# An interaction MLP in fp32 halves: rows loaded in 32-wide blocks and turned by VectorE, one spill and 16 gathers per chunk

## The chip, the cores and the metric

The kernel runs on one NeuronCore of one Trainium2 chip. The metric is the time of one execution on the device in microseconds (us), as the median over several runs. TensorE (PE) does matmuls and writes PSUM; VectorE (DVE), ScalarE (ACT) and GpSimd (POOL) do elementwise work; SyncE (SP) issues most transfers, which run on 16 DMA engines.

## The reference

It is the top of a recommendation model, for 2048 samples. Each sample has 27 feature rows of 128 numbers (`bottom_output`) and one dense row of 128.

```python
dots = jnp.einsum('bfd,bgd->bfg', bottom_output, bottom_output)
pairs = dots[:, _TRIL_I, _TRIL_J]                 # 351 = 27*26/2 per sample
x = jnp.concatenate([bottom_mlp_output, pairs, pad], axis=1)      # 128 + 351 + 1 = 480
for w, b in ((w0, b0), (w1, b1), (w2, b2), (w3, b3)):             # 480-1024-1024-512-256
    x = jax.nn.relu(x @ w.T + b)
y = x @ w_out.T + b_out                                           # 2048 x 1
```

Everything is float32.

## The kernel before

**Precision.** Each float32 operand is kept as two parts in the format fp32r: a high part (the value rounded) and a low part (value minus high part). A product is three matmuls: weight high with input high, weight high with input low, weight low with input high.

**Chunks.** The batch is cut into 8 chunks of 256 samples. A chunk has 16 units of 16 samples (4 groups of 4 samples). While chunk c goes through the layers, the units of chunk c+1 are prepared between its matmuls. The loop over c = 1 to 6 runs chunks of the same shape; chunk 0 also turns most of the weights, and chunk 7 prepares nothing.

**A unit, before.** SP loads 16 samples into a slot of `rows` (ring of 4): 108 partitions, one per (sample of the group, feature), with 4 x 128 numbers each (`load_rows`, L386). TensorE turns them by four transposes into a bank of `turned_ps` (`turn`, L546). ScalarE copies out the high part (`turned_hi`, L718), VectorE the low part (`turned_lo`, L828), into `xt`. Four Gram matmuls (`gram`, L602) give high x high and high x low of 4 samples at a time; of each 128x128 result the four diagonal 27x27 blocks count, one in each quadrant of 32 partitions. ScalarE copies quadrants 0 to 2 to `parts` (`gram_parts`, L730), VectorE quadrant 3 (`last_part`, L848). VectorE transposes the high x low part (`turn_low`, L862), and GpSimd adds the three terms (`add_parts`, L479 and L486) into `grams`.

**Spill and gather.** When the 16 units of a chunk are summed, SP writes the four quadrants of `grams` to DRAM (`blocks`), one transfer each (`spill`, L400), and then gathers the 351 pairs, one feature pair per partition, in the order of the reference: 28 transfers of 1 to 26 partitions with runs of 64 numbers (`gather_piece`, L346). Behind the gathers SP issues the rows of units 0 to 3 of the next chunk; the other 12 follow in the next chunk, each when the unit four before it is turned. ScalarE and VectorE split the gathered `pairs` into parts of the input tile x0 (`pairs_hi` L753, `pairs_lo` L904).

**The order within a chunk.** `chunk_steps` writes out one list of steps, which every engine walks in order. The steps "mm" are the products (`products`, L635), in tiles of m: 8 tiles of 12 matmuls in layer 0, 8 of 24 in layer 1, 4 of 24 in layer 2, 2 of 12 in layer 3, 408 in all. Each tile fills one of two banks of `acc`; ScalarE drains it with bias and ReLU into `h_full` (ring of 2; `drain`, L743) and VectorE splits that (`split`, L870 high and L872 low). A product group waits for the drain of the group two before it, a drain for the split of the one two before. Within layers 0 and 1 a hook comes after every HOOK = 9 matmuls; each takes the next entry of `unit_steps`: turn unit n, sum unit n-3, Gram of unit n-2. So 18 hooks end after 162 matmuls. In chunk 0 the hooks come every 6 matmuls, weights are turned in many of them, and the units' places start at hook 12. The step "pairs", the split of the next chunk's gathered pairs, stands ahead of layer 3; on ScalarE it lies ahead of the drains of layer 3. In layer 0 the first tile's product k waits for the part k of x0.

**The prologue.** Chunk 0's 16 units are turned and multiplied in plain float32 (`turn_early`, `gram_early`), W0's eight tile rows are turned by TensorE (L541) and split by ScalarE (L693, L694), then come spill and gather, 16 transfers on SP and 12 on ScalarE. W0 is loaded by two transfers of 0.96 MB.

**PSUM.** Eight banks: 2 for `acc`, 2 for `turned_ps`, 4 for Grams.

Of the kernel before, what the change touches and what calls it, by code (L numbers as in the profile page):

```python
# [14 lines left out]
P = 128  # L15
# [5 lines left out]
GROUP = 4  # L21
# [12 lines left out]
K_LAST = LAYERS[0][0] - 3 * P  # L34
# [49 lines left out]
def pair_pieces():  # L84


    out = []
    for a in range(1, FEATS):
        q, b = a * (a - 1) // 2, 0
        while b < a:  # L90
            n = min(a - b, P - (q + b) % P)
            out.append((a, b, n, q + b))
            b += n
    return out


PIECES = pair_pieces()
PIECES_OF = [sum(q // P == t for _, _, _, q in PIECES) for t in range(3)]


def unit_steps(n):


    steps, g = [], n - XT_LAG
    if n < UNITS:
        steps.append(("turn", n))
    if g >= 1:
# [25 lines left out]
def first_hooks():  # L133


    places = [FIRST_UNIT + 2 * i for i in range(4)] + [FIRST_UNIT + 8 + 4 * i // 3 for i in range(UNITS + XT_LAG - 4)]
# [11 lines left out]
def chunk_steps(gram, first=False):  # L148
# [4 lines left out]
    hooks = first_hooks() if first else [unit_steps(u) for u in range(UNITS + XT_LAG)] if gram else []  # L153
# [3 lines left out]
    for layer in range(3):  # L157
        for m in range(M_TILES[layer]):
# [4 lines left out]
            while k < K_TILES[layer]:  # L163
# [17 lines left out]
def dlrm_program(nc, x, x_mlp, w0, b0, w1, b1, w2, b2, w3, b3, w_out, b_out, y):  # L181
    weights = [w0, w1, w2, w3]
    biases = [b0, b1, b2, b3]
    with ExitStack() as ctx:
# [19 lines left out]

        h_a = sb("h_a", [P, 8, 2, CHUNK], F32R)
# [4 lines left out]
        rows = sb("rows", [P, ROWS_RING, UNIT_GROUPS, DIM])  # L210
        mlp_rows = sb("mlp_rows", [P, 2, P])
# [7 lines left out]
        stage_small = sb("stage_small", [24, P])  # L219
# [10 lines left out]
        w0_loaded = [sem(f"w0_loaded{i}") for i in range(2)]  # L230
# [7 lines left out]
        pairs_zeroed = sem("pairs_zeroed")  # L238
        xt_zeroed = sem("xt_zeroed")
# [4 lines left out]
        turned = sem("turned")  # L244
        xt_hi_done = sem("xt_hi_done")
# [4 lines left out]
        last_part_done = sem("last_part_done")  # L250
# [14 lines left out]
        weighted_done = sem("weighted_done")  # L265
# [7 lines left out]
        x_view = x.rearrange("(c u j s) f d -> c u (s f) j d", u=UNITS, j=UNIT_GROUPS, s=GROUP)  # L273
# [17 lines left out]
        out_bank = turned_ps[0:1, OUT_UNIT % TURN_RING, 0:CHUNK]  # L291

        def in_tile(layer, k, part):
            kk = K_LAST if layer == 0 and k == 3 else P
            src = x0 if layer == 0 else h_b if layer == 2 else h_a
            return src[0:kk, k, part, :]

        def weight(part, layer, m, k):
            kk = K_LAST if layer == 0 and k == 3 else P
            t = TILE0[layer] + m * K_TILES[layer] + k  # L300
            return part[0:kk, t * P:(t + 1) * P]
# [26 lines left out]

        def turned_cols(u):
# [41 lines left out]
        def _(sp):  # L371
# [6 lines left out]
            def load_rows(d, u):  # L378
# [13 lines left out]
            def spill(d):  # L392
# [56 lines left out]
            gather(0, [piece for i, piece in enumerate(PIECES) if i % 7 not in (1, 3, 5)])  # L449
# [15 lines left out]
        def _(pool):  # L465
# [5 lines left out]
            nc.gpsimd.memset(pairs[:], 0.0).then_inc(pairs_zeroed, 1)  # L471

            def add_parts(d, u):
# [4 lines left out]
                pool.wait_ge(last_part_done, n)  # L478
# [11 lines left out]
            def chunk(d):  # L490
                for u in range(UNITS):
                    add_parts(d, u)

            chunk(1)
            with pool.Fori(2, CHUNKS) as d:
                chunk(d)
# [3 lines left out]
        def _(pe):  # L500
            def turn_weights(n):
# [473 lines left out]
```

## Time and profile before

| | |
|---|---|
| median of 3 runs | 562.57 us (562.24 to 564.08) |
| profiled execution: own time | 563.71 us |
| profiled execution: span from first to last instruction | 561.9 us |
| granted TensorE clock, mean over the span | 0.989 |
| TensorE busy | 538.7 us (96%), 4521 matmuls |
| VectorE busy | 323.1 us (57%) |
| ScalarE busy | 295.5 us (53%) |
| GpSimd busy | 101.0 us (18%) |
| DMA packets | 76532, 47.49 MB, 15194 of them under 512 B |

Busy TensorE is a modelled value, since matmuls overlap: the time from one to the next is the better measure. Times of the trace are counted from the start of the span. In a row such as `205.84 1.08 PE acc L635 x9` the first number is the start and the second the length; L635 is line 635 of the kernel before.

### The profile page before, as it was taken

What the parts mean: (1) busy time and instruction counts of PE and PEld (TensorE: products, weight loads), DVE (VectorE), ACT (ScalarE), POOL (GpSimd) and SP (SyncE); (2) the same over time, 40 slices, a digit from 0 to 9 for tenths busy, and PEclk for the clock granted to TensorE, in tenths of its full rate; (3) what the DMA queues carried; (4) which work ended last, traced back from release to release, by engine and by line L of the source; (5) the groups of instructions that cost most, each with busy time, mean ns of one, the idle gap of its engine ahead of it and who ended that gap; (6) DMA issues with size and microseconds to landing.
All of it is one profiled execution on the core that took longest, in us unless ns stands there. A gap on an engine that the chain in (4) does not pass through costs nothing.

```text
span 561.9 us, 13936 instructions
## 1 busy us (share of the span) xinstructions
PE 538.7 (96%) x4521; PEld 531.7 (95%) x4521; DVE 323.1 (57%) x814; ACT 295.5 (53%) x740; POOL 101.0 (18%) x231
## 2 busy tenths in 40 slices
PE   6857999999999999999999999999999999999996
PEld 6847999999999999999999999999999999999996
DVE  3656878647842587237852588337862588325222
ACT  4535788528841588127841488227851488314112
POOL 0000044002430045002430044101430044100000
PEclk9996999999999999999999999999999999999999
DMA  9978131133213230233312231133311331100000
GB/s 233 278 268 273 43 111 40 61 93 112 81 54 81 66 112 29 65 86 98 91 53 59 75 116 37 62 89 90 99 51 37 93 111 47 59 20 2 1 1 1
DMA packets 76532, 47.49 MB, mean 85 GB/s; under 512 B 15194, under 2 KB 73850, under 8 KB 76506
## 3 DMA queue, kind: packets, MB, share of 16 engines
q1 hardware_dynamic: 75801, 47.00, 28.5%
q8 instruction: 15, 0.25, 0.2%
q10 hardware_dynamic: 705, 0.16, 0.2%
q14 instruction: 11, 0.09, 0.0%
HBM read 41.16 MB, written 5.98 MB: 84 GB/s over the span
## 4 chain that ended last, share of the span: by engine, by line
PE 82%; ACT 0%; DVE 0%; issue 0%; POOL 0%; ACTq 0%; POOLq 0%
PE acc L635 65%; PE gram_ps L602 9%; PE turned_ps L546 7%; PE gram_ps L541 1%; PE turned_ps L648 0%; PE turned_ps L611 0%; ACT parts L730 0%; ACT y_row L760 0%; DVE low_t L888 0%; ACT h_full L743 0%; DVE h_a L893 0%; POOL grams L486 0%; DVE h_a L891 0%; ACTq L728 0%; POOLq L482 0%
## 5 line engine op out<-in xcount | busy, mean ns | idle before, releaser
L635 PE MATMUL acc<-h_a,w_hi 128*128 128x256 f32 x1152 | 211.9, 284 | 0.0
L743 ACT ACTIVATE h_full<-acc,small_t 128x256 f32<-128x256 f32 x176 | 83.5, 474 | 182.2 <-PE acc L635 179.6
L635 PEld LDWEIGHTS acc<-h_a,w_hi 128*128 128x128 f32 x1152 | 179.1, 191 | 0.1
L635 PE MATMUL acc<-h_a,w_lo 128*128 128x256 f32 x576 | 162.9, 283 | 0.0
L730 ACT ACTIVATE parts<-gram_ps 27x216 f32<-27x216 f32 x336 | 114.4, 341 | 26.4 <-POOL grams L486 21.1
L635 PEld LDWEIGHTS acc<-h_a,w_lo 128*128 128x128 f32 x576 | 110.3, 192 | 0.0
L635 PE MATMUL acc<-x,w_hi 128*128 128x256 f32 (+1 forms) x512 | 99.5, 291 | 8.5 <-DVE x L904 8.5
L479 POOL TENSOR_TENSOR parts<-parts 128x128 f32<-128x128 f32 x112 | 52.3, 467 | 272.7 <-DVE parts L848 201.5
L635 PE MATMUL acc<-h_b,w_hi 128*128 128x256 f32 x512 | 93.4, 284 | 0.0
L635 PEld LDWEIGHTS acc<-x,w_hi 128*128 128x128 f32 (+1 forms) x512 | 80.0, 193 | 9.8 <-DVE x L904 8.7
L602 PE MATMUL gram_ps<-xt 128*128 128x256 f32 x448 | 80.1, 301 | 0.7 <-issue 0.6
L635 PEld LDWEIGHTS acc<-h_b,w_hi 128*128 128x128 f32 x512 | 79.7, 192 | 0.0
L828 DVE TENSOR_TENSOR xt<-turned_ps,xt 128x432 fp32r<-128x432 f32 x112 | 68.1, 608 | 18.3 <-ACT xt L718 16.0
L870 DVE CAST h_a<-h_full 128x256 fp32r<-128x256 f32 x96 | 28.9, 301 | 82.8 <-ACT h_full L743 82.2
L635 PE MATMUL acc<-x,w_lo 128*128 128x256 f32 (+1 forms) x256 | 72.9, 285 | 0.0
L635 PE MATMUL acc<-h_b,w_lo 128*128 128x256 f32 x256 | 72.4, 283 | 0.0
L718 ACT ACTIVATE xt<-turned_ps 128x432 fp32r<-128x432 f32 x112 | 59.3, 529 | 19.2 <-PE turned_ps L546 18.3
L870 DVE CAST h_b<-h_full 128x256 fp32r<-128x256 f32 x64 | 21.8, 340 | 82.1 <-ACT h_full L743 82.1
L486 POOL TENSOR_TENSOR grams<-parts,low_t 128x108 f32<-128x108 f32 x112 | 48.2, 430 | 106.4 <-DVE low_t L862 103.1
L546 PE MATMUL turned_ps<-ident,rows 108*128 108x108 f32 x464 | 62.2, 256 | 2.0 <-DMA rows<-in_r_bottom_output_dram 1.7
L602 PEld LDWEIGHTS gram_ps<-xt 128*128 128x128 f32 x448 | 60.4, 190 | 1.9 <-issue 1.9
L546 PEld LDWEIGHTS turned_ps<-ident,rows 108*128 108x128 f32 x464 | 49.7, 140 | 3.2 <-DMA rows<-in_r_bottom_output_dram 1.9
(49 smaller groups left out, 465.7 us busy)
## 6 DMA issues: line engine op xcount, KB each, us to landing
rows<-in_r_bottom_output_dram SPq DMA_DIRECT2D x112, 216.0 KB
w_raw<-in_L_rec_w_dram SPq DMA_DIRECT2D x6, 1024.0 KB, 7.5
blocks<-grams SPq DMA_DIRECT2D x32, 182.2 KB
early_rows<-in_r_bottom_output_dram SPq DMA_DIRECT2D x12, 224.0 KB, 6.2
w_raw<-in_L_rec_w_dram SPq DMA_DIRECT2D x2, 960.0 KB, 9.8
mlp_rows<-r_bottom_mlp_output_dram SPq DMA_DIRECT2D x8, 128.0 KB, 4.0
rows<-in_r_bottom_output_dram SPq DMA_DIRECT2D x4, 224.0 KB, 7.5
w_raw<-in_L_rec_w_dram SPq DMA_DIRECT2D x1, 512.0 KB, 9.5
```

What stands on the lines that cost most here:

```text
L479: nc.gpsimd.tensor_tensor(hh, hh, hl, ALU.add).then_inc(sum_done, 1)
L486: nc.gpsimd.tensor_tensor(grams[:, :, u * UNIT_GROUPS:(u + 1) * UNIT_GROUPS].rearrange("p g j -> p j g"), parts[:, u % 2, 0, :, 0:FEATS], ...
L541: last = nc.tensor.transpose(bank[0:kk, k * P:(k + 1) * P], src[:, at:at + kk], ident[:])
L546: last = nc.tensor.transpose(turned_ps[:, u % TURN_RING, j * GROUP_ROWS:(j + 1) * GROUP_ROWS], src[0:GROUP_ROWS, j, :], ident[0:GROUP_ROWS ...
L602: last = nc.tensor.matmul(gram_ps[:, u % GRAM_RING * GRAM_BANKS + j // 2, at:at + 2 * P], xt[:, u % XT_RING, j, 0], xt[:, u % XT_RING, j]. ...
L635: last = nc.tensor.matmul(acc_slot(slot), weight(wp, layer, m, k), in_tile(layer, k, xp), start=(k == 0 and n == 0), stop=(k == K_TILES[la ...
L718: nc.scalar.activation(xt_part(u, 0), turned_cols(u), ACT.Copy).then_inc(xt_hi_done, 1)
L730: last = nc.scalar.activation(parts[quad_of(s), u % 2, :, :, 0:FEATS], gram_found(u, s), ACT.Copy)
L743: nc.scalar.activation(h_full[:, slot % 2, :], acc_slot(slot), ACT.Relu, bias=small_t[:, slot:slot + 1]).then_inc(drained, 1)
L828: nc.vector.tensor_tensor(xt_part(u, 1), turned_cols(u), xt_part(u, 0).bitcast(F32), ALU.subtract).then_inc(xt_done, 1)
L870: nc.vector.tensor_copy(high, full).then_inc(high_done, 1)
```

## The change

**Rows.** From chunk 1 on, a unit is loaded by four transfers, one for each quarter q of the 128 columns: partition 32 q + f holds, for feature f (and five rows of the next sample, unused), the 32 columns of that quarter of 16 samples, in runs of 32 numbers. VectorE's transpose works on blocks of 32x32, so one instruction on 128x512 numbers gives the turned unit, in a new tile `raw` of SBUF (`turn_raw`, a new step "raw" one hook ahead of "turn"). TensorE's `turn` is gone. ScalarE takes the high part and VectorE the low part from `raw`.
**Quadrants.** ScalarE copies all four quadrants of a Gram, `last_part` is gone.
**Hooks.** HOOK is 15, and there are 19 hooks, which end after 285 matmuls. In chunk 0 the units' places start at hook 11.
**Spill and gather.** `grams` keeps all 128 partitions (the unused five of each quadrant are zeroed once), `blocks` has 32 rows per quadrant, and one transfer spills it. The pairs stand in another order, a band of the 27x27 square read in runs of constant length (9 x 14, 4 x 14, 5 x 13, 8 x 13), so four pieces of four transfers gather them; the fourth tile of x0 now has all 128 rows, the unused ones with zero weights.
**W0.** Its pair columns are loaded to `stage_pairs` in one transfer, and GpSimd copies them to `w_raw` in the band order by 71 copies of runs and one for the pad column. Its dense columns are another transfer. TensorE's first transpose of W0 waits for both.
**The rest.** GpSimd walks the same list of steps. In the prologue SP issues 8 gathers and ScalarE 8. The out row is computed at the second hook (30 matmuls) and the semaphores of splits and weighing are counted apart.

```diff
-HOOK, FIRST_HOOK = 9, 6
-GATHER_AFTER, FIRST_UNIT, LATE_HOOK = 6, 12, 38
...
+HOOK, FIRST_HOOK = 15, 6
+GATHER_AFTER, FIRST_UNIT, LATE_HOOK = 6, 11, 38
...
 EARLY_SLOTS = 8
+RAW_RING = 2
 EARLY_XT = 2 * XT_RING
-ACT_QUADS, EARLY_BY_ACT = 3, 1
-OUT_UNIT = 2
...
+PIECES = [(0, 9, 14, 0), (9, 4, 14, P), (13, 5, 13, P + 56), (18, 8, 13, 2 * P)]
+PIECES_OF = [sum(q // P == t for _, _, _, q in PIECES) for t in range(3)]
+BAND = [(q + i * nk, nk) for f, nf, nk, q in PIECES for i in range(nf)]
...
 def unit_steps(n):
-    steps, g = [], n - XT_LAG
+    steps, g = [], n - 1 - XT_LAG
     if n < UNITS:
-        steps.append(("turn", n))
+        steps.append(("raw", n))
+    if 1 <= n <= UNITS:
+        steps.append(("turn", n - 1))
     if g >= 1:
         steps.append(("sum", g - 1))
     if g >= 0:
@@ -111,6 +126,9 @@
     if g == UNITS - 1:
         steps.append(("sum", g))
...
+        block_dims = [[FEATS * DIM, UNIT_GROUPS * GROUP], [1, QUAD]]
+        x_blocks = [bass.AP(x.tensor, QUAD * q, [[step_c, CHUNKS], [step_u, UNITS], [DIM, QUAD]] + block_dims)
+                    for q in range(DIM // QUAD)]
...
-        blocks = nc.dram_tensor("blocks", (GROUP, FEATS, FEATS, RUN), F32).ap()
-        pair_rows = blocks.rearrange("s f g r -> f g s r")
+        blocks = nc.dram_tensor("blocks", (GROUP, QUAD, FEATS, RUN), F32).ap()
...
-        def gather_piece(engine, a, b, n, q):
-            dst = pairs[q % P:q % P + n, q // P, :].rearrange("p (s r) -> p s r", s=GROUP)
-            engine.dma_start(dst, pair_rows[a, b:b + n]).then_inc(gathered[q // P], 16)
+        def gather_piece(engine, f, nf, nk, q):
+            for s in range(GROUP):
+                src = bass.AP(blocks.tensor, (s * QUAD * FEATS + (FEATS + 1) * f + 1) * RUN,
+                              [[(FEATS + 1) * RUN, nf], [RUN, nk], [1, RUN]])
+                engine.dma_start(pairs[q % P:q % P + nf * nk, q // P, s * RUN:(s + 1) * RUN], src).then_inc(gathered[q // P], 16)
...
-                    sp.wait_ge(turned, d * UNITS + u + 1 - ROWS_RING)
+                    sp.wait_ge(raw_turned, (d - 1) * UNITS + u + 1 - ROWS_RING)
...
-                sp.dma_start(rows[0:GROUP_ROWS, r], x_view[d, u]).then_inc(rows_loaded[r], 16)
+                for q in range(DIM // QUAD):
+                    dst = rows[QUAD * q:QUAD * (q + 1), r].rearrange("p j (a i) -> p (j a) i", i=QUAD)
...
+                    else:
+                        sp.dma_start(dst, x_blocks[q][d, u]).then_inc(rows_loaded[r], 16)
...
-                for s in range(GROUP):
-                    sp.dma_start(blocks[s], grams[quad_of(s)]).then_inc(spilled, 16)
+                sp.dma_start(blocks.rearrange("s f g r -> (s f) (g r)"), grams[:, :, :].rearrange("p g r -> p (g r)")).then_inc(spilled, 16)
             def gather(d, pieces=PIECES):
-                sp.wait_ge(spilled, (d + 1) * GROUP * 16)
+                sp.wait_ge(spilled, (d + 1) * 16)
...
             w0_rows = w0.rearrange("(m p) k -> p m k", p=P)
-            for u in range(10):
+            for u in range(8):
                 load_early(u)
-            for i in range(2):
-                sp.dma_start(raw_rows(0)[:, 4 * i:4 * i + 4, 0:LAYERS[0][0]], w0_rows[:, 4 * i:4 * i + 4, :]).then_inc(w0_loaded[i], 16)
-                load_early(10 + i)
+            sp.dma_start(stage_pairs[:, :, :], w0_rows[:, :, DIM:]).then_inc(w0_pairs_loaded, 16)
+            for u in range(8, 12):
+                load_early(u)
+            sp.dma_start(raw_rows(0)[:, :, 0:DIM], w0_rows[:, :, 0:DIM]).then_inc(w0_dense_loaded, 16)
             for u in range(12, UNITS):
                 load_early(u)
...
-            gather(0, [piece for i, piece in enumerate(PIECES) if i % 7 not in (1, 3, 5)])
+            gather(0, PIECES[0::2])
...
             nc.gpsimd.memset(pairs[:], 0.0).then_inc(pairs_zeroed, 1)
+            nc.gpsimd.memset(grams[:], 0.0).then_inc(grams_zeroed, 1)
...
+            pool.wait_ge(w0_pairs_loaded, 16)
+            ordered = raw_rows(0)[:, :, DIM:]
+            for col, n, q, step in ROW_RUNS:
+                nc.gpsimd.tensor_copy(ordered[:, :, q:q + (n - 1) * step + 1:step], stage_pairs[:, :, col:col + n])
+            nc.gpsimd.tensor_copy(ordered[:, :, PAD_ROW:PAD_ROW + 1], stage_pairs[:, :, PAIRS:]).then_inc(w0_in_order, 1)
...
+                    if g == 0:
+                        pe.wait_ge(w0_in_order, 1)
+                        pe.wait_ge(w0_dense_loaded, 16)
...
-            def turn(d, u):
...
-                turn_rows(u, rows[:, r])
...
                 act.wait_ge(gram_done, u + 1)
+                if u == 0:
+                    act.wait_ge(grams_zeroed, 1)
                 for s in range(EARLY_BY_ACT):
...
+                act.wait_ge(raw_turned, (d - 1) * UNITS + u + 1)
...
-                nc.scalar.activation(xt_part(u, 0), turned_cols(u), ACT.Copy).then_inc(xt_hi_done, 1)
+                nc.scalar.activation(xt_part(u, 0), raw_cols(u), ACT.Copy).then_inc(xt_hi_done, 1)
...
                     act.wait_ge(grams_done, d * UNITS + u - 1)
-                for s in range(ACT_QUADS):
+                for s in range(GROUP):
                     last = nc.scalar.activation(parts[quad_of(s), u % 2, :, :, 0:FEATS], gram_found(u, s), ACT.Copy)
...
+                if slot >= 2:
+                    act.wait_ge(split_done, split_count(c, slot) - 2)
+                elif not (isinstance(c, int) and c == 0):
+                    act.wait_ge(weighed, 2 * c - 1 + slot)
...
+                    act.wait_ge(spilled, 16)
                     act.wait_ge(pairs_zeroed, 1)
-                    for piece in [piece for i, piece in enumerate(PIECES) if i % 7 in (1, 3, 5)]:
+                    for piece in PIECES[1::2]:
                         gather_piece(nc.scalar, *piece)
...
+            def turn_raw(d, u):
+                r = u % ROWS_RING
+                dve.wait_ge(rows_loaded[r], ((d - 1) * (UNITS // ROWS_RING) + u // ROWS_RING + 1) * 64)
+                dve.wait_ge(xt_done, d * UNITS + u + 1 - RAW_RING)
+                nc.vector.transpose(raw[:, u % RAW_RING].rearrange("p j n -> p (j n)"),
+                                    rows[:, r].rearrange("p j n -> p (j n)")).then_inc(raw_turned, 1)
             def turned_lo(d, u):
                 dve.wait_ge(xt_hi_done, (d - 1) * UNITS + u + 1)
-                nc.vector.tensor_tensor(xt_part(u, 1), turned_cols(u), xt_part(u, 0).bitcast(F32),
+                nc.vector.tensor_tensor(xt_part(u, 1), raw_cols(u), xt_part(u, 0).bitcast(F32),
                                         ALU.subtract).then_inc(xt_done, 1)
...
-            def last_part(d, u):
```

## Rows read from the trace of the kernel before

**Rows 1.** The page: span, busy time by engine, and traffic in 40 slices.
```profile
span 561.9 us, 13936 instructions
...
PE 538.7 (96%) x4521; PEld 531.7 (95%) x4521; DVE 323.1 (57%) x814; ACT 295.5 (53%) x740; POOL 101.0 (18%) x231
...
GB/s 233 278 268 273 43 111 40 61 93 112 81 54 81 66 112 29 65 86 98 91 53 59 75 116 37 62 89 90 99 51 37 93 111 47 59 20 2 1 1 1
```

**Rows 2.** Chain in order of time, 195 to 260: start, length, what.
```profile
205.84 1.08 PE acc L635 x9
206.92 0.37 PE turned_ps L546 x4
207.29 0.49 PE gram_ps L602 x4
...
222.10 0.71 PE gram_ps L602 x4
222.81 20.88 PE acc L635 x174
```

**Rows 3.** Windows (PE, PEld, DVE, ACT, POOL, clock, DMA): one period; chunk 0.
```profile
188.59:252.46 63.87, 63.81 (x542) 63.22 (x541) 37.92 (x97) 35.19 (x91) 14.27 (x32) 1.00 0.26 75
74.60:91.00 16.40, 16.40 (x146) 16.40 (x146) 13.49 (x33) 14.86 (x39) 7.94 (x18) 1.00 0.37 108
```

**Rows 4.** Groups of instructions, whole span: busy us, mean ns, idle before.
```profile
L730 ACT ACTIVATE parts<-gram_ps 27x216 f32<-27x216 f32 x336 | 114.4, 341 | 26.4 <-POOL grams L486 21.1 <-PE gram_ps L602 0.8
...
L828 DVE TENSOR_TENSOR xt<-turned_ps,xt 128x432 fp32r<-128x432 f32 x112 | 68.1, 608 | 18.3 <-ACT xt L718 16.0
...
L718 ACT ACTIVATE xt<-turned_ps 128x432 fp32r<-128x432 f32 x112 | 59.3, 529 | 19.2 <-PE turned_ps L546 18.3
...
L486 POOL TENSOR_TENSOR grams<-parts,low_t 128x108 f32<-128x108 f32 x112 | 48.2, 430 | 106.4 <-DVE low_t L862 103.1 <-issue 1.7
L848 DVE COPY parts<-gram_ps 27x216 f32<-27x216 f32 x112 | 43.5, 388 | 3.6 <-PE gram_ps L602 0.2
L872 DVE TENSOR_TENSOR h_a<-h_full,h_a 128x256 fp32r<-128x256 f32 x96 | 43.4, 452 | 3.3
L862 DVE STREAM_TRANSPOSE low_t<-parts 128x128 f32<-128x128 f32 x112 | 34.0, 303 | 6.2 <-ACT parts L730 5.1 <-issue 0.5
L870 DVE CAST h_a<-h_full 128x256 fp32r<-128x256 f32 x96 | 28.9, 301 | 82.8 <-ACT h_full L743 82.2
...
L743 ACT ACTIVATE h_full<-acc,small_t 128x256 f32<-128x256 f32 x176 | 83.5, 474 | 182.2 <-PE acc L635 179.6
...
L753 ACT ACTIVATE x<-pairs 128x256 fp32r<-128x256 f32 x24 | 8.4, 408 | 2.4 <-DMA pairs<-blocks 2.3
...
L748 ACT ACTIVATE x<-turned_ps 128x256 fp32r<-128x256 f32 x8 | 3.0, 377 | 0.0
```

**Rows 5.** Timeline of SP's queue, 218 to 250: start, length over all, issues.
```profile
225.46 2.22 SPq L400 DMA_DIRECT2D blocks<-grams  x4
230.68 10.87 SPq L346 DMA_DIRECT2D pairs<-blocks  x28
241.84 2.29 SPq L386 DMA_DIRECT2D rows<-in_r_bottom_output_dram  x4
```

**Rows 6.** DMA, 237.8 to 239.6 (gathers; 40 slices), then 246 to 248 (rows).
```profile
GB/s 51 80 34 11 0 12 0 0 17 23 17 11 17 17 17 23 17 51 51 80 74 74 17 17 23 40 29 17 17 17 17 23 17 17 17 17 17 17 17 17
...
DMA packets 819, 0.40 MB, mean 201 GB/s; under 512 B 34, under 2 KB 819, under 8 KB 819
...
q1 hardware_dynamic: 819, 0.40, 70.9%
```

**Rows 7.** Timelines of GpSimd, SP's queue and TensorE in the prologue.
```profile
1.42 0.74 POOL L471 MEMSET pairs<- 128x768 f32 x1
...
36.73 6.29 SPq L346 DMA_DIRECT2D pairs<-blocks  x16
...
45.57 0.80 PE L635 MATMUL acc<-x,w_hi 128*128 128x256 f32 x2 [8.49 <-DVE x L904]
```

More of the change, by code:

```diff
@@ L78, in slot_of, with band_of_rows @@
     return FIRST_SLOT[layer] + m
-def pair_pieces():
+PIECES = [(0, 9, 14, 0), (9, 4, 14, P), (13, 5, 13, P + 56), (18, 8, 13, 2 * P)]
+PIECES_OF = [sum(q // P == t for _, _, _, q in PIECES) for t in range(3)]
+BAND = [(q + i * nk, nk) for f, nf, nk, q in PIECES for i in range(nf)]
+PAD_ROW, TILE_ROWS = 2 * P + 8 * 13, [9 * 14, 4 * 14 + 5 * 13, 8 * 13 + 1]
+assert sum(nk for _, nk in BAND) == PAIRS and len(BAND) == FEATS - 1
+def band_of_rows():
     out = []
     for a in range(1, FEATS):
-        q, b = a * (a - 1) // 2, 0
+        place = []
+        for b in range(a):
+            flat = min(x for x in (b * FEATS + a, a * FEATS + b) if 1 <= x % (FEATS + 1) <= BAND[x // (FEATS + 1)][1])
+            place.append(BAND[flat // (FEATS + 1)][0] + flat % (FEATS + 1) - 1)
+        b = 0
         while b < a:
-            n = min(a - b, P - (q + b) % P)
-            out.append((a, b, n, q + b))
+            n = 1
+            while b + n < a and place[b + n] - place[b + n - 1] == (place[b + 1] - place[b]) > 0:
+                n += 1
+            out.append((a * (a - 1) // 2 + b, n, place[b], place[b + 1] - place[b] if n > 1 else 1))
             b += n
     return out
-PIECES = pair_pieces()
-PIECES_OF = [sum(q // P == t for _, _, _, q in PIECES) for t in range(3)]
+ROW_RUNS = band_of_rows()
+assert len({q + i * d for _, n, q, d in ROW_RUNS for i in range(n)}) == PAIRS
 def unit_steps(n):
-    steps, g = [], n - XT_LAG
+    steps, g = [], n - 1 - XT_LAG
     if n < UNITS:
-        steps.append(("turn", n))
+        steps.append(("raw", n))
+    if 1 <= n <= UNITS:
+        steps.append(("turn", n - 1))
     if g >= 1:
@@ L133, in first_hooks @@
 def first_hooks():
-    places = [FIRST_UNIT + 2 * i for i in range(4)] + [FIRST_UNIT + 8 + 4 * i // 3 for i in range(UNITS + XT_LAG - 4)]
+    places = [FIRST_UNIT + 2 * i for i in range(4)] + [FIRST_UNIT + 8 + 4 * i // 3 for i in range(UNIT_HOOKS - 4)]
     hooks = [[] for _ in range(LATE_HOOK + W_GROUPS - LATE_WEIGHTS)]
@@ L152, in chunk_steps @@
     steps, done = [], 0
-    hooks = first_hooks() if first else [unit_steps(u) for u in range(UNITS + XT_LAG)] if gram else []
+    hooks = first_hooks() if first else [unit_steps(u) for u in range(UNIT_HOOKS)] if gram else []
     every = FIRST_HOOK if first else HOOK
@@ L229, in dlrm_program @@
         small_loaded = sem("small_loaded")
-        w0_loaded = [sem(f"w0_loaded{i}") for i in range(2)]
+        w0_pairs_loaded = sem("w0_pairs_loaded")
+        w0_in_order = sem("w0_in_order")
+        w0_dense_loaded = sem("w0_dense_loaded")
         w1_loaded = [sem(f"w1_loaded{i}") for i in range(4)]
@@ L488, in add_parts, with chunk @@
                     parts[:, u % 2, 0, :, 0:FEATS], low_t[:, u % 2, :, 0:FEATS], ALU.add).then_inc(grams_done, 1)
[L490 to L496, printed above, removed]
+            def chunk(c):
+                for step in chunk_steps(True, isinstance(c, int) and c == 0):
+                    if step[0] == "sum":
+                        add_parts(c + 1, step[1])
+            chunk(0)
+            with pool.Fori(1, CHUNKS - 1) as c:
+                chunk(c)
         @block.tensor
@@ L538, in turn_weights @@
                 for k in range(4):
-                    kk = K_LAST if layer == 0 and k == 3 else P
                     at = (4 * part + k) * P
-                    last = nc.tensor.transpose(bank[0:kk, k * P:(k + 1) * P], src[:, at:at + kk], ident[:])
+                    last = nc.tensor.transpose(bank[:, k * P:(k + 1) * P], src[:, at:at + P], ident[:])
                 last.then_inc(w_turned, 1)
@@ L607, in turn_mlp @@
                 pe.wait_ge(mlp_loaded, (d + 1) * 16)
-                pe.wait_ge(xt_done, (d + 1) * UNITS)
+                if isinstance(d, int) and d == 0:
+                    pe.wait_ge(xt_done, UNITS)
+                else:
+                    pe.wait_ge(mlp_done, d)
                 for t in range(2):
@@ L836, in early_rest @@
                 last.then_inc(grams_done, 1)
-            def last_part(d, u):
-                dve.wait_ge(gram_done, d * UNITS + u + 1)
-                if isinstance(d, int) and d == 1 and u < 2:
-                    dve.wait_ge(parts_zeroed, 1)
-                else:
-                    dve.wait_ge(grams_done, d * UNITS + u - 1)
-                for s in range(ACT_QUADS, GROUP):
-                    last = nc.vector.tensor_copy(parts[quad_of(s), u % 2, :, :, 0:FEATS], gram_found(u, s))
-                last.then_inc(last_part_done, 1)
             def turn_low(d, u):
```

95 lines of the change are left out of this document (40 added, 55 removed).

## The prediction

> **What bounds the kernel now.** I read the page's head first: TensorE is busy for 96% of the span, VectorE for 57%, ScalarE for 53% [rows 1]. Then the chain of waits in order of time, inside a chunk of the loop: it alternates between nothing but TensorE pieces. Nine product matmuls take 1.08 us, the four transposes of a unit 0.37, its four Gram matmuls 0.49; without units 174 products run through in 20.88 us, 0.12 us each [rows 2]. The windows say the same by stage: one chunk period is 63.87 us with TensorE busy for 63.81 of them, VectorE for 37.92, ScalarE for 35.19 [rows 3]. So what leaves TensorE's queue shortens the run one for one, until another engine, the rows' transfers or the spill and gather can't keep up. The last two have cover now: units end after 162 of a chunk's 408 products, and 30 us lie between the last Gram (222.10) and the next chunk's first product at 252.46 [rows 2, 3].
>
> **The change, part by part.** The sum is made against the profiled execution's own time, 563.7 us (561.9 span [rows 1] and 1.8 around it); the median of the runs is 562.6, 1.1 lower.
>
> *Transposes off TensorE.* Chunks 1 to 7 have 16 units each, turned while chunks 0 to 6 run. Per chunk 16 x 0.37 = 5.9 us go, so a period of 63.87 becomes 57.95. Over all 112 units that is 41 us, the most there is to gain in the chunks.
>
> *VectorE.* Per chunk it loses the fourth quadrant's copy, 16 x 0.388 = 6.2 us, and gets 16 transposes of 128x512. The trace has only the 128x128 one, 0.303 us [rows 4]. Bounds: 0.50 us if each further element costs half a nanosecond, 1.21 if cost grows in proportion. Between L872 (256 elements, 0.452) and L828 (432, 0.608) an element costs 0.9 to 1.0 ns, so I take 0.303 + 384 x 1.05 = 0.70 us: 11.2 per chunk. L828 now reads SBUF instead of PSUM; L872, from SBUF, lies on the same line, so I leave it at 0.61. The whole is 37.9 [rows 3] - 6.2 + 11.2 = 43 us of 58. The tight place is layer 0. There TensorE needs 96 x 0.12 + 3 Grams x 0.49 = 13.0 us, and VectorE has 6 transposes (4.2), 5 low parts (3.05), 2 small transposes (0.6), 8 splits (0.30 + 0.45 each, 6.0) and the last chunk's weighing (1.5): 15.4. It ends some 2.4 us behind; layer 1 asks for the eighth split only at its eighth k, 7 x 0.36 + 0.49 = 3.0 us in, so the lag just fits. I put 0 on it. At 1.21 us per transpose the lag is 3 us longer, and 3.5 us a chunk are lost.
>
> *ScalarE.* It takes the fourth quadrant: 16 x 0.34 = 5.5 us more per chunk. In layer 1 hooks now come every 15 products, so every 15 x 0.12 + 0.49 = 2.29 us, and each brings four quadrants (1.38), one high part (0.53) and 15/24 of a drain (0.30): 2.21. That is 97%, with semaphore gaps about all of it. What waits behind it: the next Gram waits for the copies of two units before, and each products group for a drain. I put 0.3 us per chunk on this, bounds 0 and 2.
> The high part now reads SBUF. The trace has both sources at 256 elements: 0.407 from SBUF (L753), 0.377 from PSUM (L748) [rows 4]; 0.03 us more per hook still fits into 2.29.
> The Trainium skill (VectorE: DVE Perf Modes, the section on the TRN2 errata) says that a ScalarE instruction with an SBUF source pays a fixed extra, 224 against 172 cycles, 43 ns as an estimate. It speaks against this move, the trace agrees in direction with 30 ns, and by the page's figure a hook would need 2.25 us and still fit.
>
> *The hooks end later.* The last Gram stands after 285 of a chunk's 408 products instead of 162. From it to the next chunk's first product, which waits for the drain of (3, 0), which ScalarE does behind its three copies of the gathered pairs, TensorE has 0.49 + 123 x 0.12 + 0.3 = 15.5 us. What must fit: Gram to spill issue, 3.4 us before (222.10 to 225.46) [rows 2, 5], 3.2 with no unit close before it; the spill, 5.2 us before as four issues (2.22) on it, as one 3.8 (bounds 3 and 5.2); the gathers, issued at 10.87/28 = 0.39 us each, 16 of them 6.2 us; the last one's landing 2 (in the prologue the last issue ends at 43.0 and TensorE goes on at 45.6, with a copy and a low part of 0.4 each in between [rows 7]); ScalarE's copy and drain 0.41 + 0.47. Sum 16.1: TensorE stands 0.6 to 0.7 us per chunk (bounds 0 and 4.5, the latter if a gather of three levels takes 0.6 to issue). The 28 gathers and four spills of before needed 22 us on the same path and cost nothing under 30 us of cover.
>
> *Rows in blocks.* A unit is now four transfers of 512 runs of 128 B, 2048 packets instead of 432 of 512 B. What one packet costs: 819 packets of 512 B kept 16 engines 70.9% busy for 2 us, 27.7 ns each or 18.5 B/ns; in a gather, the long stretches at a constant 17 GB/s are one engine working alone, 15 ns per 256 B packet [rows 6]. On this line a packet of 128 B costs 9 ns. Bounds for it: 9, and 27.7 if size doesn't help at all; the nearest row is the 256 B one, so I reckon with 9 to 15, 1.2 to 1.9 us per unit over 16 engines, below the 2.29 of a hook. SP issues 16 transfers for the first four units behind the gathers, at 0.57 us each in the loop (2.29 us for four [rows 5]) or 0.39 at best. The last gather is issued 13.2 us after the last Gram (3.2 + 3.8 + 6.2); four issues (2.3), the transfer (1.3) and latency (2) bring the first unit's rows at 18.8, and VectorE wants them at 16.2 + 1.8 = 18.0. It waits 0.5 to 0.8 us in the stage where it already lags, about as much as that lag's slack (3.0 - 2.4), so I put 0 on this too.
>
> *Chunk 0.* Its hooks come every 6 products with 4 units on 3 tiles: before, 1.82 us per unit (9 units in 16.4 us), VectorE busy for 13.5 and ScalarE for 14.9 of them [rows 3]; TensorE's part is the same 1.45 + 0.37. After, ScalarE needs 1.38 + 0.53 + a third of 0.47, with gaps 2.15: 16 x 0.33 = 5.3 us more, less 1.3 for starting a hook earlier. So +4 (bounds -3 and +8): here the change loses.
>
> *Prologue.* TensorE stands 8.49 us until the pairs of chunk 0 arrive; SP issues 16 gathers in 6.29 us [rows 7] and ScalarE 12. Now each issues 8, 3.1 us; with the single spill (0.7 earlier) the pairs come 3.5 us sooner. Against it, GpSimd puts W0's columns into band order by 72 copies of 8 x 352 elements in all. Its only single-source row is a memset, 0.74 us for 768 elements [rows 7]: by that 2.7 us of elements and some 0.1 per copy, 10 us; at the 0.43 us of an add of 108 elements (L486 [rows 4]) 31 us. Ahead of the pair columns' 1.4 MB eight units of 0.23 MB are in the queue, 3.2 MB at some 260 GB/s [rows 1] and 2 us of latency, so they land at about 15 and all is ready between 25 and 46; I take 15 us of copies, so 30, just before TensorE comes to it at 31.5. Prologue -3.5 (bounds -4.5 and +11).
>
> **Sum.** Chunks 1 to 6: 6 x (-5.92 + 0.7 + 0.3) = -29.5. Chunk 0 +4, prologue -3.5, chunk 7 nothing: -29. 563.7 - 29 = 534.7 of the profile, about 534 as a median.
>
> **Rivals.** (a) *The small packets bind*, the slower side. From a unit's turn to the next chunk's first rows nothing can be loaded for some 19 us (Gram and sums, spill, gathers), so a chunk needs 16 T + 19, T being a unit's transfer. It decides against the forecast from T = 2.4 us (19 ns a packet), and against the kernel before from T = 2.8 us (22 ns). If a 128 B packet costs what a 512 B one does, T = 3.55, a chunk 76 us and the run 7 x 12 = 84 us longer: 646. For it: no packet of 128 B is in the trace, and no more than 0.41 packets per ns are moved in any row (819 in 2 us). Against: the 256 B rate of 17 B/ns [rows 6]. Chance 0.15.
> The Trainium skill (DMA: Bandwidth & Descriptors, Specifications) asks for at least 512 B for line rate, since below it the engine reads, modifies and writes. That is rule (a); the trace's 256 B packets, at 17 against 18.5 B/ns, don't show it.
> (b) *The tail is longer*: gathers at 0.6 us or rows behind them late, 4 us more per chunk: 534 + 24 = 558. For it: the issues of rows in the loop take 0.57 and more. Chance 0.12.
> (c) *VectorE or ScalarE binds*: transposes of 1.2 us, or ScalarE over 100% in layer 1, 3 us per chunk and 3 in chunk 0: 555. For it: the 97%. Chance 0.13.
> (d) *All of it is hidden*, chunk 0 too: 562.6 - 41 - 4 = 518. Against: ScalarE's load in chunk 0. Chance 0.10.
>
> **How the numbers follow.** The forecast has 0.50, its own range is 525 to 546. 518 to 566 holds all but (a) and the ends of (b) and (c), some 0.18. A measurement here tells 0.3%, 1.7 us, from no change: faster 0.79, same 0.04, slower 0.17, most of the last from (a).
>
> **What would show it.** In the changed trace: a unit's chain piece without L546; a period near 59 us; L862-like transposes of 128x512 at 0.70; the gap of TensorE before a chunk's first product 0.7 us with ScalarE's drain or the copy of pairs as releaser; no wait of VectorE for rows over 1 us; in chunk 0 TensorE waiting for ScalarE's copies; the first products at about 42 instead of 45.6. Waits of the transposes for rows in every unit would mean (a); a period of 62 with ScalarE without idle, (c).

## The result, and the profile after

The changed kernel takes 579.25 us (median; 575.11 to 580.27), the kernel before 563.33 in the same job: ratio 1.027, 95% interval 1.0215 to 1.0325. The change makes it 2.7% slower, where I had forecast 534 us and a range up to 566. The forecast was wrong in sign. The profiled execution took 579.57 us.

The page of the changed kernel, answering [rows 1]:

```profile
span 577.8 us, 13768 instructions
...
PE 509.6 (88%) x4073; PEld 500.5 (87%) x4073; DVE 336.1 (58%) x806; ACT 335.9 (58%) x844; POOL 126.9 (22%) x307
...
PEclk9987999999999799998999899998999899997999
...
PE 35%; ACT 14%; DVE 12%; issue 11%; SPq 11%; DMA 9%; POOL 4%; ACTq 2%; DVEq 1%; POOLq 0%
```

TensorE has 29 us less to do, and the run is 16 us longer: TensorE stands. The last line is the chain that ended last. SP's queue (issuing DMAs) and DMA hold 20% of it; before, TensorE had 82% and they none worth a line. The clock row dips at the starts of chunks 2 to 7, not at that of chunk 1.

The list of waits says where TensorE stands (who waits, for whom, us in total, times, longest):

```profile
ACT x L788 <- DMA pairs<-blocks: 36.6, 13, 5.1
...
PE acc L671 <- ACT h_full L778: 32.3, 6, 7.1
...
PE acc L671 <- DVE x L930: 8.7, 1, 8.7
...
PE acc L671 <- DVE h_b L897: 6.0, 6, 1.2
```

Six times, at the starts of chunks 2 to 7, the first product waits for ScalarE's drain (chunk 1 starts without a wait); ScalarE does that drain behind the copies of the gathered pairs, and stands at those for the gathers. The chain of waits in order of time (start, length, what), from the spill on, answers to the tail of [rows 2]:

```profile
242.94 3.50 DMA blocks<-grams
246.45 0.84 SPq L378
247.34 0.75 SPq L378
...
249.69 0.66 SPq L378
...
252.37 0.74 SPq L378
...
255.43 0.69 SPq L378
...
257.58 2.05 DMA pairs<-blocks
259.98 0.47 ACT h_full L778
```

The chain again, its TensorE pieces behind the wait (a piece ends with the end of its last matmul, and two small transposes lie between these):

```profile
260.56 5.49 PE acc L671 x30
266.28 3.60 PE acc L671 x30
```

SP's queue in the same stretch, to be held against [rows 5]:

```profile
242.94 0.35 SPq L438 DMA_DIRECT2D blocks<-grams  x1
246.45 11.78 SPq L378 DMA_DIRECT2D pairs<-blocks  x16
258.53 8.46 SPq L426 DMA_DIRECT2D rows<-in_r_bottom_output_dram  x16
```

Sixteen gathers take 11.8 us to issue, more than the 28 of before (10.9): 0.74 us each against 0.39. Windows of one period and of its first 3.6 us, with the columns of [rows 3]:

```profile
260.50:326.30 65.80, 59.39 (x476) 58.80 (x476) 40.16 (x97) 41.17 (x108) 16.03 (x32) 0.97 0.48 85
260.50:264.10 3.60, 3.54 (x16) 3.54 (x17) 1.58 (x5) 0.77 (x2) 0.00 (x0) 0.50 0.79 123
```

Chunk 1 starts at 128.42 and chunk 7 at 521.08, so a period is 65.4 us on average, against 58.95 forecast. The one of the window, 260.56 to 326.32, is 65.8: 57.75 of work (57.95 forecast; the first experiment shows it without the rest), 5.15 of waiting for the drain at its end, 1.2 of waiting for a split, and 1.65 at its start. There the granted clock is 0.50 (1.2 GHz) for the first 3.6 us, and the first 30 products take 5.49 us; without the long wait before them they take 3.85 (first experiment).

The groups that answer to [rows 4]:

```profile
L762 ACT ACTIVATE parts<-gram_ps 27x216 f32<-27x216 f32 x448 | 152.5, 340 | 25.2 <-POOL grams L533 18.6 <-PE gram_ps L634 1.8
...
L861 DVE STREAM_TRANSPOSE raw<-rows 128x512 f32<-128x512 f32 x112 | 77.8, 695 | 0.1
...
L526 POOL TENSOR_TENSOR parts<-parts 128x128 f32<-128x128 f32 x112 | 64.5, 576 | 240.2 <-ACT parts L762 239.9
L866 DVE TENSOR_TENSOR xt<-raw,xt 128x432 fp32r<-128x432 f32 x112 | 64.3, 574 | 3.8 <-ACT xt L750 3.6
L750 ACT ACTIVATE xt<-raw 128x432 fp32r<-128x432 f32 x112 | 62.7, 560 | 3.1 <-DVE raw L861 2.2
...
L518 POOL COPY w_raw<-stage_pairs 128x32 f32<-128x32 f32 (+8 forms) x71 | 11.4, 237 | 12.2 <-DMA stage_pairs<-in_L_rec_w_dram 12.2
```

The idle column of L861 is 0.1 us for all 112 turns: they never wait for rows. DMA while rows are loaded (280 to 306), where [rows 6] had gathers:

```profile
DMA packets 15541, 1.93 MB, mean 74 GB/s; under 512 B 15541, under 2 KB 15541, under 8 KB 15541
...
q1 hardware_dynamic: 15541, 1.93, 47.5%
```

47.5% of 16 engines' 26 us over 15541 packets is 12.7 ns for one of 128 B. The prologue, answering [rows 7]; first SP's and ScalarE's queues:

```profile
37.52 6.29 SPq L378 DMA_DIRECT2D pairs<-blocks  x8
```
```profile
37.53 6.43 ACTq L378 DMA_DIRECT2D pairs<-blocks  x8
```

and TensorE's first products of chunk 0:

```profile
45.77 0.79 PE L671 MATMUL acc<-x,w_hi 128*128 128x256 f32 x2 [8.72 <-DVE x L930]
```

Eight issues take what sixteen took, so nothing is won there either.

### The profile page after: what moved, and what is told of

Same layout as the page of the kernel before. It is cut to its first block, busy times and chain, and to the rows that moved or that the text cites. A ratio compares the mean times of both kernels' runs of the same rounds, so it can differ in the third digit from the quotient of the medians.

```text
span 577.8 us, 13768 instructions
## 1 busy us (share of the span) xinstructions
PE 509.6 (88%) x4073; PEld 500.5 (87%) x4073; DVE 336.1 (58%) x806; ACT 335.9 (58%) x844; POOL 126.9 (22%) x307
## 4 chain that ended last, share of the span: by engine, by line
PE 35%; ACT 14%; DVE 12%; issue 11%; SPq 11%; DMA 9%; POOL 4%; ACTq 2%; DVEq 1%; POOLq 0%
PE acc L671 29%; SPq L378 11%; ACT parts L762 9%; DMA blocks<-grams 5%; POOL grams L533 4%; ACT h_full L778 4%; DVE xt L866 3%; DVE raw L861 3%; DMA pairs<-blocks 2%; DMA early_rows<-in_r_bottom_output_dram 2%; DVE h_b L895 2%; PE gram_ps L634 2%; PE gram_ps L588 2%; DVE low_t L888 2%; PE gram_ps L617 2%
## 5 line engine op out<-in xcount | busy, mean ns | idle before, releaser
L762 ACT ACTIVATE parts<-gram_ps 27x216 f32<-27x216 f32 x448 | 152.5, 340 | 25.2 <-POOL grams L533 18.6
L671 PE MATMUL acc<-x,w_hi 128*128 128x256 f32 x512 | 107.3, 308 | 41.0 <-ACT h_full L778 32.3
L671 PEld LDWEIGHTS acc<-x,w_hi 128*128 128x128 f32 x512 | 88.9, 214 | 42.8 <-issue 28.3
L526 POOL TENSOR_TENSOR parts<-parts 128x128 f32<-128x128 f32 x112 | 64.5, 576 | 240.2 <-ACT parts L762 239.9
L634 PE MATMUL gram_ps<-xt 128*128 128x256 f32 x448 | 73.1, 285 | 7.9 <-ACT parts L762 4.0
L861 DVE STREAM_TRANSPOSE raw<-rows 128x512 f32<-128x512 f32 x112 | 77.8, 695 | 0.1
L671 PE MATMUL acc<-x,w_lo 128*128 128x256 f32 x256 | 77.3, 302 | 0.0
L866 DVE TENSOR_TENSOR xt<-raw,xt 128x432 fp32r<-128x432 f32 x112 | 64.3, 574 | 3.8 <-ACT xt L750 3.6
L750 ACT ACTIVATE xt<-raw 128x432 fp32r<-128x432 f32 x112 | 62.7, 560 | 3.1 <-DVE raw L861 2.2
L671 PEld LDWEIGHTS acc<-x,w_lo 128*128 128x128 f32 x256 | 54.3, 212 | 0.0
```

The lines of the kernel that those rows point to most:

```text
L526: nc.gpsimd.tensor_tensor(hh, hh, hl, ALU.add).then_inc(sum_done, 1)
L634: last = nc.tensor.matmul(gram_ps[:, u % GRAM_RING * GRAM_BANKS + j // 2, at:at + 2 * P], xt[:, u % XT_RING, j, 0], xt[:, u % XT_RING, j]. ...
L671: last = nc.tensor.matmul(acc_slot(slot), weight(wp, layer, m, k), in_tile(layer, k, xp), start=(k == 0 and n == 0), stop=(k == K_TILES[la ...
L750: nc.scalar.activation(xt_part(u, 0), raw_cols(u), ACT.Copy).then_inc(xt_hi_done, 1)
L762: last = nc.scalar.activation(parts[quad_of(s), u % 2, :, :, 0:FEATS], gram_found(u, s), ACT.Copy)
L861: nc.vector.transpose(raw[:, u % RAW_RING].rearrange("p j n -> p (j n)"), rows[:, r].rearrange("p j n -> p (j n)")).then_inc(raw_turned, 1)
```

## The experiments

**What was to be told apart.** The 45 us between forecast and result could have several causes. First, the tail is set by the time that the gathers take to issue, and an issue is dear because its two sides are cut differently: nested rows of DRAM (9 x 14) against one run of partitions (126). Its rivals: the price belongs to something else in the tail (the spill, the landing, the bytes); the late hooks are to blame, and earlier ones would bring the gain back, or else only move the loss, since ScalarE and VectorE can't follow; and what decides is the lost cover, so that the kernel before would stand as well with hooks so late. The expectations number them. Each run was timed beside the kernel before (563.7 to 564.3 us).

**A quarter of the gathers.** Only those of the first sample quarter, 4 of 16; three quarters of the pairs aren't gathered.

```diff
-            for s in range(GROUP):
+            for s in range(1):
...
```

> The changed kernel with only 4 of its 16 gathers per chunk (those of the first sample of each group; the other three quarters of the pairs stay as they were, so this leaves work out). Theory I (SyncE's issue of the gathers, 0.74 us each instead of 0.39, is what TensorE waits for at each chunk's start): 12 issues fewer are 8.8 us, the path from last Gram to first product falls under its cover, the wait of 5.0 us and the low clock behind it go; period 58.5 to 60 us instead of 65.5, the start of the first chunk 4 us earlier; the run 536 (530 to 542). Rival II (the late first product comes from units that end late, or from rows): the wait stays above 3 us, 560 or more.

Measured: 533.4 us (532.1 to 534.2), ratio 0.9455 [0.9431, 0.9479]. SP's queue:

```profile
229.78 0.35 SPq L438 DMA_DIRECT2D blocks<-grams  x1
233.30 3.06 SPq L378 DMA_DIRECT2D pairs<-blocks  x4
```

and one period in the columns of [rows 3]:

```profile
242.44:301.44 59.00, 57.75 (x476) 57.16 (x477) 40.29 (x96) 41.12 (x107) 15.57 (x32) 1.00 0.51 90
```

An issue costs the same when only four follow each other (0.77), so the price isn't that of a queue filling up. The spill is the same too (3.5). With 12 issues fewer the wait and the low clock are both gone, and 46 us with them; the period is 59.0, 57.75 of them TensorE's work and 1.25 its wait for one split. The gathers carry the whole miss; whether by their issue or by what they move, the last experiment tells.

**By rows.** 26 transfers, one for each feature, all four sample quarters at once; both sides are cut alike (partitions, quarters, run).

```diff
-            for s in range(GROUP):
-                src = ... [[(FEATS + 1) * RUN, nf], [RUN, nk], [1, RUN]]
+            for i in range(nf):
+                src = ... [[RUN, nk], [QUAD * FEATS * RUN, GROUP], [1, RUN]]
...
```

> The changed kernel with the same pairs gathered by 26 transfers, one per feature row, each with the same three dimensions on both sides (13 or 14 partitions, 4 runs, 64 numbers), instead of 16 whose DRAM side is nested and whose SBUF side is not. Theory Ia (the unequal shapes make an issue dear): 0.39 us per issue, 26 are 10.1 instead of 11.8 us, 1.7 less per chunk; the run 567 (560 to 572). Rival Ib (any transfer out of the band costs 0.7 us to issue): 19 us, 7 more per chunk, 625 or more.

Measured: 575.5 us (573.8 to 577.1), ratio 1.0219 [1.0193, 1.0245]. It lies outside the 560 to 572 expected.

```profile
244.59 10.93 SPq L380 DMA_DIRECT2D pairs<-blocks  x26
```

0.42 us each instead of 0.74, as the first theory has it, but 26 of them: only 0.85 us shorter per chunk, six times 5.1 us, and the span fell by 5.8. The wait was still 3.9 to 6.1 us, and the first 30 products behind it still took 5.2 to 6.1, so what the low clock costs stayed. The median is 4 us lower where 12 were expected, and the intervals of the two ratios overlap (1.0215 to 1.0325 for the changed kernel): what this run shows is the price of an issue, not a gain.

**Hooks every 12 products.** The last Gram comes 57 products earlier.

```diff
-HOOK, FIRST_HOOK = 15, 6
+HOOK, FIRST_HOOK = 12, 6
```

> The changed kernel with hooks every 12 products instead of 15, so that the last Gram stands at 228 instead of 285 and 6.8 us more of products cover spill and gathers. Theory III (units are themselves bound at some 2.2 us by ScalarE and VectorE, so the preparing of a chunk is one chain of 42 + 21 us and earlier hooks only move the waits): period 64.3, no long wait and no low clock at the chunk's start, but TensorE waits at the Grams; the run 567 (562 to 572). Rival IV (only the cover was short): period 58 to 60, 540.

Measured: 564.3 us (562.4 to 566.9), ratio 1.0013 [0.9991, 1.0034], no difference from before. TensorE, its Grams:

```profile
225.16 0.73 PE L634 MATMUL gram_ps<-xt 128*128 128x256 f32 x4 [0.30 <-DVE xt L866]
...
227.38 0.74 PE L634 MATMUL gram_ps<-xt 128*128 128x256 f32 x4
...
229.85 0.74 PE L634 MATMUL gram_ps<-xt 128*128 128x256 f32 x4 [0.31 <-DVE xt L866]
```

Two units take 4.69 us where 2 x (12 x 0.12 + 0.49) = 3.9 would do: a unit costs ScalarE and VectorE 2.35 us, and TensorE now stands at its Grams. The period is 63.3 on average. The wait in the tail is gone and has become this one: where the hooks end can't be bought back by placing them closer.

**The kernel before with hooks every 15.**

```diff
-HOOK, FIRST_HOOK = 9, 6
+HOOK, FIRST_HOOK = 15, 6
```

> The kernel before with hooks every 15 products: transposes stay on TensorE, 4 spills and 28 gathers, last Gram at 270 of 408. Theory V (the later last Gram alone uncovers the path, which takes 22 us there against 17 of cover): TensorE waits some 5 us per chunk and runs 2 us at the low clock behind it, 6 x 7 = 41 us and 3 in chunk 7: 604 (595 to 612). Rival VI (the path of before has room): 563.

Measured: 595.5 us (594.6 to 596.5), ratio 1.0558 [1.0535, 1.058]. Its waits and SP's queue:

```profile
PE acc L635 <- ACT h_full L743: 23.0, 6, 4.0
```
```profile
244.38 2.21 SPq L400 DMA_DIRECT2D blocks<-grams  x4
249.61 10.93 SPq L346 DMA_DIRECT2D pairs<-blocks  x28
```

The same wait at the same place: some 22 us from the last Gram to the pairs are free under 30 us of cover and cost 32 us of run when the hooks end late. Spill and gather of before were no cheaper, they were hidden.

**By rows, on two queues.** The 26 transfers again, 14 issued by SP and 12 by ScalarE between its drains of layer 2, where it has room.

```diff
+TILE_OF = [[row for row in ALL_ROWS if row[2] // P == t] for t in range(3)]
+BY_SP = TILE_OF[0][:5] + TILE_OF[1][:5] + TILE_OF[2][:4]
+BY_ACT = [TILE_OF[0][5:] + TILE_OF[1][5:6], TILE_OF[1][6:] + TILE_OF[2][4:6], TILE_OF[2][6:]]
...
+                    elif step[0] == "fetch":
+                        for row in BY_ACT[step[1]]:
+                            gather_row(nc.scalar, *row)
```

> The changed kernel, hooks at 15, with the 26 transfers by feature row of e2, 14 issued by SyncE and 12 by ScalarE between its drains in layer 2; all pairs are gathered. Theory I (issue time of the gathers on one queue is the whole of the wait): 14 x 0.42 = 5.9 us of issues instead of 11.8, the path falls to 16.8 us under 16.7 of cover, as with e1; period 59.0 to 59.5, no low clock behind the start; the run 535 (531 to 541). Rival VII (what costs is the transfers' own work, so a second queue doesn't help): 565 or more.

Measured: 539.65 us (538.7 to 541.7), ratio 0.9566 [0.9533, 0.96]. SP's and ScalarE's queues, then TensorE's first product of the next chunk:

```profile
239.14 5.86 SPq L392 DMA_DIRECT2D pairs<-blocks  x14
```
```profile
239.64 2.10 ACTq L392 DMA_DIRECT2D pairs<-blocks  x5
...
242.66 2.06 ACTq L392 DMA_DIRECT2D pairs<-blocks  x5
...
245.54 0.73 ACTq L392 DMA_DIRECT2D pairs<-blocks  x2
```
```profile
248.96 0.50 PE L689 MATMUL acc<-x,w_hi 128*128 128x256 f32 x2 [0.68 <-ACT h_full L796]
```

The two queues issue side by side. From the last Gram (231.01) to this product it is 17.95 us, 4 less than in the changed kernel and still 1.9 above the forecast; TensorE has work or its wait for the split in all but 0.7 of them. The periods average 59.6. This kernel computes all of the reference and beats both others: 4.3% under the one before.

**Both: two queues and hooks every 12.** The line of the third experiment on this kernel.

> e5 with hooks every 12 products. Theory III (with hooks at 12 the units alone bind, at 2.35 us each, and the 180 products behind them add 21.6 us whatever the gathers cost): as e3, period 64, the run 560 to 565, 25 to 30 us slower than e5. Rival IV (e3 was still held by its gathers): as e5, 535.

Measured: 560.45 us (558.8 to 562.9), ratio 0.9945 [0.9918, 0.9973]. With the tail short the units bind just as before (4.68 us for two Grams). 15 is the better place once the gathers are quick.

**A quadrant back to VectorE, hooks every 12.** The third experiment's kernel, with VectorE copying the fourth quadrant.

```diff
-HOOK, FIRST_HOOK = 15, 6
+HOOK, FIRST_HOOK = 12, 6
...
-                for s in range(GROUP):
+                for s in range(ACT_QUADS):      # 3; VectorE copies the fourth
...
```

> e3 (hooks at 12, 16 gathers) with the fourth quadrant's copy back on VectorE. Theory VIII (VectorE and ScalarE are both near 2.3 us a unit; per pair of units VectorE then has 2 x (0.70 + 0.57 + 0.30 + 0.39) + 0.74 = 4.7 us, what a pair takes now): no gain, 564 (560 to 572). Rival IX (ScalarE alone holds the units): a pair falls to 3.9, the pace of the products, the period to 58 to 60 and the run to 540.

Measured: 562.3 us (560.0 to 565.1), ratio 0.9967 [0.9943, 0.9992]. Its waits:

```profile
PE gram_ps L639 <- DVE parts L893: 31.3, 57, 1.3
```

Two units take 4.55 us instead of 4.69, and the releaser is VectorE now. Both engines are near 2.3 us a unit; moving a copy between them gives 0.07 us a unit.

**The kernel before with one spill.** Its four spill transfers become one on 128 partitions.

```diff
-                for s in range(GROUP):
-                    sp.dma_start(blocks[s], grams[quad_of(s)]).then_inc(spilled, 16)
+                sp.dma_start(blocks..., grams...).then_inc(spilled, 16)
...
```

> The kernel before with the one spill of 128 rows (and grams zeroed once), all else as it was. Theory: 3.5 us instead of 5.2 from issue to landing, under cover in every chunk: 563, within 0.3%; at most 1.5 us off in the prologue.

Measured: 562.2 us (560.9 to 566.7), ratio 0.9976 [0.9948, 1.0004]: no difference that can be told. From issue to the first gather it is 3.5 us instead of 5.2, under cover.

**A flat shape.** The test of the first theory by itself: 16 gathers as in the changed kernel, same partitions, same packets and bytes, but the DRAM side is one run of neighbouring rows, as long as the partitions. It fetches other rows than the pairs.

```diff
-                              [[(FEATS + 1) * RUN, nf], [RUN, nk], [1, RUN]])
+                              [[RUN, nf * nk], [1, RUN]])
```

> The changed kernel with its 16 gathers, the same partitions and the same 1404 packets of 256 B, but the DRAM side read as one run of rows (126, 56, 65 and 104 neighbouring rows) instead of nested runs of 14 or 13 rows, so that both sides have the same shape. It gathers other rows than the pairs, so the output leaves the reference. Theory Ia (the unequal shapes of the two sides make an issue dear): 0.31 to 0.42 us per issue, 16 in 5 to 7 us, the wait at the chunk's start gone, period 59, the run 535 to 541. Rival X (the number of packets or of partitions sets it): 0.74 us as now, 579.

Measured: 538.0 us (536.0 to 540.4), ratio 0.952 [0.9466, 0.9574].

```profile
234.75 0.36 SPq L437 DMA_DIRECT2D blocks<-grams  x1
238.26 6.70 SPq L377 DMA_DIRECT2D pairs<-blocks  x16
```

0.42 us each. One level less on one side of the transfer, with the same partitions, packets and bytes, is 5.1 us of issuing a chunk, and 41 us of run against the changed kernel. One wait is left, 1.8 us at the start of chunk 2; the 30 products behind it take 3.85.

## Why the prediction was wrong

The step that failed is the tail, "16 gathers, issued at 10.87/28 = 0.39 us each, 6.2 us". They took 11.8, 0.74 each. The 0.39 is the price of the transfers of before, whose two sides are cut alike; the new ones lay 9 x 14 rows of DRAM on 126 partitions, and no row of the trace had that shape. I saw the risk and put it into the bounds at 0.6, which was no measured end: it was the 0.57 of the rows' issues. Rival (b) has the mechanism with a chance of 0.12, but at 4 us a chunk where 6.5 were lost. A second term was at nothing without a reason: what TensorE's clock costs behind a wait.

Step by step, for the tail from the last Gram (238.49) to the next first product (260.56), 22.1 us where 16.1 were forecast. TensorE covers 17.1 of them (15.5 forecast; 1.2 of the difference is a wait for a split), and the rest is the wait of 5.0:
- Gram to spill issue 4.45 instead of 3.2 us. ScalarE has four quadrants of each of the last two units to copy (1.4 us a unit), waits for GpSimd in between, and GpSimd's last two sums follow. 1.2 us short; it also delays VectorE's last small transpose, behind which the next split waits, so that TensorE stands up to 1.2 us at `h_b`.
- The spill 3.5 (3.8 forecast): near.
- The issues 11.8 instead of 6.2: the miss. A wait of 5.0 us instead of 0.7 follows.
- The last landing: 2.05 from the start of its issue, and so 1.4 behind the end of the issues, where the sum has 2; 0.6 too much. ScalarE's copy and drain 0.9, as forecast.
- What no step had: behind that wait the granted clock is 0.50, and the first 30 products take 5.1 to 6.0 us instead of 3.85, 6.5 in chunk 7. In the first experiment and in the flat shape, with no long wait, the clock's row stays whole and the same 30 take 3.85.

The books: the profiled 579.6 is 44.9 above the 534.7 that the forecast gives for the profile. Six periods at 65.4 instead of 58.95 are 38.7; the first products at 45.8 instead of 42 are 3.7, again by eight issues at 0.8 (6.3 us) where 3.1 were forecast; chunk 7's slow start is 2.7. Sum 45.1, so it closes to 0.2. Two experiments show it: with a quarter of the gathers 533.4, with the flat shape 538.0, against 534 forecast.

The other steps, from the same traces:
- *Transposes off TensorE*: right. TensorE's work in a period is 57.75 us (57.95 forecast), and with a short tail the periods average 59.0 to 59.7 (58.95 forecast, but there with 0.7 at the drain and 0.3 for ScalarE, here mostly with 1.25 at a split).
- *VectorE*: 0.70 forecast, 0.695 measured; in chunks 1 to 6 TensorE has no wait in layer 0 behind the first product.
- *ScalarE*: 97% of a hook forecast in layer 1; over eight hooks there (273.7 to 292.0) it is busy for 16.68 of 18.3 us, 91%, gaps left out. TensorE's waits at the Grams, 7.9 us in the whole run (4.0 for its copies, 3.0 for VectorE, 1.0 without a releaser), all lie in chunk 0; in chunks 1 to 6 there is none, where 0.3 us each were forecast. Right at 15 products a hook; the third experiment shows how near the edge it is, 2.35 us a unit against a hook of 2.29. The high part from SBUF took 560 ns against 529 before, 31 more as the 256-element rows had it. The Trainium skill (VectorE: DVE Perf Modes, the section on the TRN2 errata) would have 43, an estimate from its cycles: the direction holds, the size is smaller.
- *Rows in blocks*: 12.7 ns a packet in the bounds of 9 to 15, no wait: rival (a), which held most of my chance of slower, is refuted. The run was slower for the cause I had priced at 558. The Trainium skill (DMA: Bandwidth & Descriptors, Specifications) asks for at least 512 B for line rate. By this trace the rate is indeed lower, 10 B/ns against 18.5 for 512 B, but a packet of 128 B doesn't cost as much as one of 512 B.
- *Chunk 0*: +4 forecast, 3.7 measured (82.65 us from its first product to that of chunk 1, against 78.95).
- *GpSimd's copies*: 15 us forecast, 11.4 measured; ready at 27.6, hidden as said.
- *Rivals*: (c) didn't happen at this hook distance, (d) neither.

**What stays open.** Why the unequal cut is dear. Single issues of the four pieces took 0.77 (9 x 14 rows, 126 packets), 0.63 (4 x 14, 56), 0.72 (5 x 13, 65) and 0.67 us (8 x 13, 104) on average, by an issue's own length (from start to start it is some 0.04 more), so it isn't the packets: 56 of them cost more here than 126 in the flat shape (0.38). Nor is it the number of levels, since the transfers by rows have three on both sides and take 0.38. The Trainium skill (DMA: Bandwidth & Descriptors, the section on why a DMA increments its semaphore by 16) says that a transfer is spread over the largest number of engines up to 16 that divides the slowest dimension of both sides. By that the pieces use 9, 4, 5 and 8 engines and the flat ones 14, 14, 13 and 13, so the flat shape changes this too. But the kernel before has transfers with both sides alike that by the same rule use as few. Its issues of 4, 5, 8, 9 and 17 partitions, the last on one engine by that rule, with 68 packets:

```profile
232.12 0.28 SPq L346 DMA_DIRECT2D pairs<-blocks  x1
232.44 0.30 SPq L346 DMA_DIRECT2D pairs<-blocks  x1
233.47 0.30 SPq L346 DMA_DIRECT2D pairs<-blocks  x1
233.82 0.31 SPq L346 DMA_DIRECT2D pairs<-blocks  x1
237.26 0.26 SPq L346 DMA_DIRECT2D pairs<-blocks  x1
```

So few engines don't make an issue dear by themselves, and the cut is what remains; what the queue does with it no trace shows. Equal cuts aren't always cheap either: in every chunk one issue of before, the first of 20 partitions, takes 0.56 to 1.09 us (0.74 at 238.33), and the second of 20 mostly 0.28. That too stays open.

## What to carry to other kernels

The price of issuing a DMA belongs to its shape: before merging transfers, look whether both sides stay cut alike, and where no row of the trace has the new shape, give the issue at least twice the known price in the range and see what the cover says to it. Fewer transfers isn't the aim; time on the issuing queue is, and a second queue with room halves it (539.7 us here with 26 transfers, 579.3 with 16). When work moves later in a period, list everything that had been free under the cover, and price the wait together with what it does to TensorE's clock behind it (here 1.2 to 2.7 us a time on top of waits of about 5).

## What the runs showed of the hardware

- An issue from SP or ScalarE took 0.74 to 0.8 us on average with the DRAM side in two levels of rows against one of partitions, and 0.39 to 0.42 with both sides cut alike; with the same partitions, packets and bytes 0.74 against 0.42.
- After a wait of 5.0 us TensorE's clock was granted at 0.50 (1.2 GHz) and 30 products took 5.49 us; after 0.7 us (two queues) and 1.8 us (flat shape, chunk 2) they took 3.84 and 3.85.
- GpSimd's add of 128x128 (L526) took 576 ns against 467 before, beside other instructions of VectorE; whether they are the cause wasn't tested. Its 71 copies of 8 to 96 numbers a partition took 11.4 us, 0.16 each from start to start.
- A spill of 864 KB from 128 partitions lands in 3.5 us as one transfer; four of 27 partitions each, 729 KB together, had taken 5.2.
